# Folding low-rank factors into the weight tiles of one feed-forward, and a late place for the last out products of two others

## The chip, the cores and the metric

One core of one Trainium2 chip runs the whole program; the other cores do nothing. The metric is the time of one execution on the device in microseconds (us). It is the median over runs; the kernel before was run three times, from 2981.08 to 2985.95 us.

The engines are TensorE (PE: matrix products, with the weight loads shown apart as PEld), VectorE (DVE), ScalarE (ACT), GpSimd (POOL) and SyncE (SP, which here issues the transfers). PSUM is eight banks of 128 x 512 float32, which PE writes and DVE and ACT read.

## What is computed

The reference is a chain of eight stages over x of 8 x 128 x 512: four attentions and four feed-forwards, each with a LayerNorm ahead and a residual add behind:

```
x = x + L0_xattn(layernorm(x), ...)      stage 0
x = x + L0_ffn(layernorm(x), ...)        stage 1   (F0)
x = x + L1_xattn(layernorm(x), ...)      stage 2
x = x + L1_ffn(layernorm(x), ...)        stage 3   (F1)
x = x + L2_xattn(...); x + L2_ffn(...)   stages 4, 5
x = x + L3_xattn(layernorm(x), ...)      stage 6
x = x + L3_ffn(layernorm(x), ...)        stage 7   (F3)
```

The feed-forward of stage 1 is the one whose arithmetic is rearranged. Its hidden width is 1376 (padded to 11 blocks of 128) and the rank of its factors is 16:

```
def _lora_linear(x, w, a, b):
    base = jnp.einsum('bsd,od->bso', x, w)
    low = jnp.einsum('bsr,or->bso', jnp.einsum('bsd,rd->bsr', x, a), b)
    return base + low * SCALING          # SCALING = 2
h1 = _lora_linear(x, w1, lora_A1, lora_B1)
h3 = _lora_linear(x, w3, lora_A3, lora_B3)
g = jax.nn.silu(h1) * h3
return _lora_linear(g, w2, lora_A2, lora_B2)
```

F1 (stage 3) has 14 blocks of 128 hidden units and picks one of each 32 by a product of rank 16; F3 (stage 7) is `gelu(x @ inter_w + inter_b) @ output_w + output_b` with 16 blocks.

## The kernel before

**Data and precision.** x lies in SBUF as 8 tiles (b) of 128 x 512. A LayerNorm writes it transposed into `xnT`. Each operand of a matrix product is split into a rounded high part and the low part that is left (float32r), and a product of two such operands is three matmuls (high x high, low x high, high x low): `PASSES`, recorded at L397. So 128 x 128 weights against 512 columns, contracted over four blocks of 128, is 12 matmuls of 128x512; the 1024 columns are two halves, 24 matmuls.

**A feed-forward** (`FeedForward`, `ffn_sp`, `ffn_act`, `ffn_pool`, `ffn_pe`, `ffn_dve`) runs over chunks of 128 hidden units. For each chunk SP loads raw weight tiles of 128 x 512 into the six places of `ring`; ACT writes the high part (L1641, `ffn_act_high`) and POOL the low part (L1456, `ffn_pool_tiles`) into `w_in`, `w_kv` (two places each) or `w_out` (four places). F0 has three tiles a chunk: `in` (w1), `in2` (w3) and `out` (w2). PE makes `proj` (h1) and `score` (h3), 24 matmuls each; ACT applies silu to `proj` (L1668), DVE multiplies by `score` (L1740), and ACT and DVE split the result into `acts` (L1676, L1705). Every second chunk PE makes the out products of the two chunks before: for each of the 8 tiles of x, 6 matmuls into one of two banks `outp`, which DVE adds to x (L1700). The order on each engine is the order in which the code is written; semaphores (`m.wait(engine, event, count)`) tie the engines together.

**The low-rank part of F0 before.** `low_rank_product` multiplies A1 and A3 (loaded to `brow`, split by POOL into `w_kv[:, 1]`) with `xnT`: 24 matmuls (L413, L417) ahead of the first chunk; ACT and DVE split the result into `low_in`. Each chunk then has one more matmul for each half of `proj` (L1577) and of `score` (L1588), with the factors B1 and B3 in `low_b`. For w2, `second_low` multiplies each chunk's `acts` by A2 into two banks (L1518, 4 matmuls a chunk), and after the last chunk ACT and DVE split that sum (L1687, L1771) before each last out product gets one more matmul with B2 (L1545). The sums themselves, as L1771, wait for the last chunk.

**Around it.** `prepare_low_b` splits B1 and B3 on DVE in the first four heads of stage 0. `pe_tail`, `act_tail` and `dve_tail` are the passage from a stage to the next: the last 8 out products, the adds that also sum x (L503), squared deviations on ACT (L509), the reciprocal roots (DVE, 128x4), normalised tiles, 8 x 4 transposes (L537), and the split into `xnT`. `unread_passes` are matmuls whose result nobody reads (L593); they stand in places where PE would have nothing to do. Stage 2 starts on PE with `project_k` (L1953), which waits for normalised x from DVE (L2133).

**F1 and F3 at their end.** In F1's last chunk (13) the out products of x tiles 4 to 7 stand between `proj` and the transposes of the picks (L1599). In F3 the 8 out products of the pair before stand ahead of the last chunk's `proj` (chunk 15). The last pair's out products then open with the slot of the last chunk but one (6 matmuls for x tiles 0 and 1), and go on once the last chunk's low parts (L1705) are there.

Of the kernel before, what the change touches and what calls it, by code (L numbers as in the profile page):

```python
# [7 lines left out]
F32 = mybir.dt.float32  # L8
# [184 lines left out]
class FeedForward:  # L193


    def __init__(self, name, stage, kind, chunks, semaphores, before, small=(), row=None):
        self.name, self.stage, self.kind, self.chunks, self.row = name, stage, kind, chunks, row
        self.low_rank = kind != "gelu"
# [9 lines left out]
                      lowfull=silu, low2=2 * (kind == "silu"), low2_low=2 * (kind == "silu"),  # L208
                      low_low=4 * silu_once + 2 * pick_once, a_high=2 * silu_once + 3 * pick_once, a_split=2 * silu_once + 2 * pick_once, bmax=pick, equal=pick, weighed=pick, fmax=pick,
# [4 lines left out]
        for i in range(self.ring):  # L214
# [4 lines left out]
    NAMES = ("split high_w pre_landed pre_split small_landed sfull tfull made high low outfull added lowfull low2 "  # L219
             "low2_low low_low a_high a_split bmax equal weighed fmax picked").split() + [  # L220
# [37 lines left out]
def build(nc, ins, out):  # L258

    with ExitStack() as ctx:  # L260
# [66 lines left out]
        with nc.sbuf_tensor("low_a2", [P, 11 * 96], F32R) as low_a2, nc.sbuf_tensor("low_b2", [96, D], F32R) as low_b2:  # L327
            pass
# [38 lines left out]
        a2_raw, b2_raw = sq[:, 0:11 * 16], sq[0:96, 11 * 16:11 * 16 + D]  # L367
# [195 lines left out]
        def take_low_rank(act, A, half):  # L563
            A.events.wait(act, ("pfull", half), 1)
            if A.kind == "silu":
                act.activation(low_in[:, half * HALF:(half + 1) * HALF], proj[half][:, :], ACT.Copy, scale=2.0)\
                   .then_inc(A.events["pfree", half], 1)
                return
# [3 lines left out]
        def take_low_part(dve, A, half):  # L572
# [3 lines left out]
            if A.kind == "pick":  # L576
                dve.scalar_tensor_tensor(low_in[0:64, cols], low_in[0:64, cols].bitcast(F32), consts[0:64, C_MINUS + 1:C_MINUS + 2],
                                         proj[half][0:64, :], ALU.mult, ALU.add).then_inc(A.events["low_low"], 1)
                return
            for rows in (slice(32, 64), slice(96, 128)):  # L580
                dve.scalar_tensor_tensor(low_in[rows, cols], proj[half][rows, :], 2.0, low_in[rows, cols].bitcast(F32),
                                         ALU.mult, ALU.subtract).then_inc(A.events["low_low"], 1)

        def first_gelu_product(pe, half):

            if half == 0:
                F3.events.wait(pe, "split", F3.tile(0, 0, 0) + 1)
            pe_project_fresh(pe, F3.stage, w_in, 0, half).then_inc(F3.events["pfull", half], 1)
# [10 lines left out]
        def pe_tail(pe, n, out_of):  # L599
            for b in range(B):  # L600
                if n in LN_STAGES:
# [14 lines left out]
            for F in (F0, F1):  # L616
                if F.stage == n:
                    low_rank_product(pe, F, 0)
            if F3.stage == n:
                first_gelu_product(pe, 0)  # L620
# [7 lines left out]
        def act_tail(act, n, wait_added, first=0):  # L628
# [7 lines left out]
            for b in range(first, BH + 1):  # L636
                deviations(b)
            for b in range(2):
# [16 lines left out]
            for F in (F0, F1):  # L655
                if F.stage == n:
                    take_low_rank(act, F, 0)

        def dve_tail(dve, n, add_of):

            for b in range(BH + 1):
                add_of(b)
            if n > 7:
# [19 lines left out]
            for b in range(4, B):  # L683
                dve_ln_low(dve, n, b)


        def attention_sp(sp, A):
# [24 lines left out]
            if A.own_kv:  # L712
                sp.dma_start(sq[:, :], ins["F0_b"][:, 0:T]).then_inc(b_landed, 16)
                sp.dma_start(ring[:, 4, 0:11 * P - T], ins["F0_b"][:, T:11 * P]).then_inc(b_landed, 16)
            group(0)
# [400 lines left out]
        def attention_act(act, A):  # L1116
# [89 lines left out]
            for F in (F0, F3):  # L1206
                if F.stage == A.stage + 1:
# [1508 lines left out]
```

## Time and profile before

| | us |
|---|---|
| median of 3 runs | 2982.11 |
| lowest, highest | 2981.08, 2985.95 |
| the profiled execution: its time | 2981.35 |
| the profiled execution: its span, first to last instruction | 2979.5 |
| PE busy in the span | 2886.9 (97%) |
| DVE, ACT, POOL busy | 1705.7, 1121.6, 991.4 |
| mean granted TensorE clock, share of full | 0.998 |
| F0, from its first product to the first product of stage 2 | 889.8 to 1104.4 |

Times in the rows are microseconds from the span's start; a row of a timeline merges neighbouring instructions of one line, with their count behind an x. The last matmul's modelled end lies beyond the start of the next row, so the pace of matmuls is read from starts, not from durations. In brackets stands how long the engine had been idle and what released it.

### The profile page before, as it was taken

How to read it: one execution, taken by the hardware profiler on the slowest of the kernel's cores; microseconds unless marked ns; L12 is line 12 of the kernel's file. 1: busy time of each engine (PE TensorE's matmuls, PEld its weight loads, DVE VectorE, ACT ScalarE, POOL GpSimd, SP SyncE). 2: the span in 40 equal slices, each digit the busy share in tenths (PEclk: the TensorE clock that was granted, in tenths of full speed). 3: DMA queues.
4: the chain of work that ended last, by engine and by line, in shares of the span. 5: the costliest groups of instructions: out<-in, count | busy, mean ns of one | idle time of the engine just before them, and what ended most of it. 6: DMA issues, size and time to landing. Idle time of an engine off the chain costs nothing.

```text
span 2979.5 us, 47771 instructions
## 1 busy us (share of the span) xinstructions
PE 2886.9 (97%) x16134; PEld 2433.1 (82%) x16134; DVE 1705.7 (57%) x3462; ACT 1121.6 (38%) x3635; POOL 991.4 (33%) x830
## 2 busy tenths in 40 slices
PE   7999999999999998899999999999999999999999
PEld 6888888888888865577778888888778888888787
DVE  6545544445462249988766666666664444445644
ACT  4322222222242237732354444444443333333432
POOL 3433343423313226644333322332232333332221
PEclk9999999999999999999999999999999999999999
DMA  3111111111112111011111101110021111110111
GB/s 121 46 50 41 40 39 41 48 41 44 42 36 57 34 43 30 27 43 39 37 40 36 31 26 32 35 35 18 26 60 33 36 35 35 35 35 22 46 50 46
DMA packets 68613, 120.09 MB, mean 40 GB/s; under 512 B 8681, under 2 KB 14185, under 8 KB 68113
## 3 DMA queue, kind: packets, MB, share of 16 engines
q1 hardware_dynamic: 68498, 118.60, 13.4%
q8 instruction: 67, 1.10, 0.2%
q14 instruction: 48, 0.39, 0.0%
HBM read 116.41 MB, written 2.10 MB: 40 GB/s over the span
## 4 chain that ended last, share of the span: by engine, by line
PE 86%; DVE 8%; issue 3%; ACT 2%; POOL 1%; DMA 0%; DVEq 0%; SPq 0%; ACTq 0%; POOLq 0%
PE proj L397 40%; PE outp L397 24%; PE heado L1015 6%; PE score L974 6%; PE turn L1001 3%; PE score L397 2%; PE proj L413 1%; PE proj L941 1%; DVE blockmax L1715 1%; DVE picks L1725 1%; PE outp L1995 0%; DVE firstmax L1723 0%; PE turn L924 0%; PE proj L1958 0%; DVE acts L1705 0%
## 5 line engine op out<-in xcount | busy, mean ns | idle before, releaser
L397 PE MATMUL outp<-w_out,acts 128*128 128x512 f32 x3288 | 843.2, 400 | 13.0 <-DVE x L1700 3.9
L397 PE MATMUL proj<-xnT,w_in 128*128 128x512 f32 x3192 | 757.2, 392 | 1.3 <-ACT big L1079 1.3
L397 PEld LDWEIGHTS outp<-w_out,acts 128*128 128x128 f32 x3288 | 594.1, 188 | 144.1 <-DVE x L1700 13.0
L397 PEld LDWEIGHTS proj<-xnT,w_in 128*128 128x128 f32 x3192 | 592.6, 188 | 124.7 <-issue 1.5
L397 PE MATMUL proj<-ctxT,w_kv 128*128 128x512 f32 x1536 | 366.0, 394 | 19.8 <-POOL w_kv L731 18.6
L729 POOL TENSOR_TENSOR w_out<-ring,consts 128x512 fp32r<-128x512 f32 x96 | 102.4, 1066 | 820.9 <-PE outp L397 820.9
L397 PEld LDWEIGHTS proj<-ctxT,w_kv 128*128 128x128 f32 x1536 | 286.6, 189 | 79.1 <-issue 18.6
L1306 DVE TENSOR_TENSOR x<-x,outp 128x512 f32<-128x512 f32 x360 | 244.7, 685 | 182.2 <-PE outp L397 179.1
L1082 DVE COPY big<-proj 128x512 f32<-128x512 f32 x136 | 93.6, 688 | 343.6 <-PE proj L397 339.3
L1079 ACT ACTIVATE big<-proj 128x512 f32<-128x512 f32 x136 | 81.4, 598 | 476.4 <-PE proj L397 469.7
L729 POOL TENSOR_TENSOR w_kv<-ring,consts 128x512 fp32r<-128x512 f32 x93 | 98.0, 1053 | 464.0 <-DMA ring<-in_L_wk 445.6
L1177 ACT ACTIVATE acts<-heado 128x512 fp32r<-128x512 f32 x192 | 114.6, 597 | 309.2 <-PE heado L1015 309.2
L1312 DVE TENSOR_TENSOR acts<-heado,acts 128x512 fp32r<-128x512 f32 x192 | 132.6, 691 | 148.6 <-ACT acts L1177 148.5
L1015 PEld LDWEIGHTS heado<-ptbuf,big 128*128 128x128 f32 x1536 | 200.7, 191 | 17.8 <-ACT ptbuf L1165 1.0
L1165 ACT ACTIVATE ptbuf<-turn 128x512 f32<-128x512 f32 x192 | 114.2, 595 | 267.6 <-PE turn L1001 267.5
L1015 PE MATMUL heado<-ptbuf,big 128*128 128x128 f32 x1536 | 202.3, 274 | 1.0 <-DVE acts L1312 1.0
L974 PEld LDWEIGHTS score<-big 128*128 128x128 f32 x1536 | 184.4, 193 | 9.5 <-issue 4.7
L974 PE MATMUL score<-big 128*128 128x128 f32 x1536 | 188.9, 276 | 3.0 <-issue 1.7
L397 PE MATMUL proj<-w_kv,ctxT 128*128 128x256 f32 x1536 | 183.1, 280 | 0.9 <-DVE big L1082 0.9
L397 PEld LDWEIGHTS proj<-w_kv,ctxT 128*128 128x128 f32 x1536 | 182.0, 188 | 2.3 <-DVE big L1082 1.1
L1700 DVE TENSOR_TENSOR x<-x,outp 128x512 f32<-128x512 f32 x152 | 103.3, 685 | 89.9 <-PE outp L397 89.8
L729 POOL TENSOR_TENSOR w_in<-ring,consts 128x512 fp32r<-128x512 f32 x96 | 106.6, 1111 | 116.9 <-PE proj L397 65.8
(330 smaller groups left out, 4022.7 us busy)
## 6 DMA issues: line engine op xcount, KB each, us to landing
ring<-in_L_wq SPq DMA_DIRECT2D x96, 256.0 KB, 2.7
ring<-in_L_wo SPq DMA_DIRECT2D x96, 256.0 KB, 2.7
ring<-in_F_in SPq DMA_DIRECT2D x52, 256.0 KB, 2.7
ring<-in_L_wk SPq DMA_DIRECT2D x48, 256.0 KB, 2.7
ring<-in_L_wv SPq DMA_DIRECT2D x48, 256.0 KB, 3.4
ring<-in_F_out SPq DMA_DIRECT2D x41, 256.0 KB, 2.6
x<-in_x SPq DMA_DIRECT2D x2, 1024.0 KB, 8.4
big<-in_ctxT SPq DMA_DIRECT2D x4, 512.0 KB, 8.0
```

Of the source, the lines that this page charges most:

```text
L397: mm = pe.matmul(bank_ap, w_ap(a, c), rhs(b, c), start=first and c == 0 and n == 0, stop=last and c == chunks - 1 and n == len(PASSES) - 1)
L729: pool.tensor_tensor(dst[:, slot, 0, :], ring[:, r, :], zeros512, ALU.add).then_inc(m["high_w"], 1)
L974: mm = pe.matmul(score[half][:, b * P:(b + 1) * P], qT[:, t], kT[:, t], start=True, stop=True)
L1001: mm = pe.transpose(turn[:, b * P:(b + 1) * P], probs[j % 2][:, half, b * P:(b + 1) * P], ident)
L1015: mm = pe.matmul(heado[:, b * P:(b + 1) * P], v_pair[:, n, j % 2, :] if A.own_kv else v[:, n * S:(n + 1) * S], ptbuf[:, half, b * P:(b + 1 ...
L1079: return engine.activation(dst, src, ACT.Copy)
L1082: return engine.tensor_copy(dst, src)
L1165: act.activation(ptbuf[:, half, :], turn[:, :], ACT.Copy).then_inc(m["tfree"], 1)
L1177: act.activation(acts[:, j, 0, half * HALF:(half + 1) * HALF], heado[:, :], ACT.Copy)\
L1306: dve.tensor_tensor(x[:, b, :], x[:, b, :], outp[b % 2][:, :], ALU.add).then_inc(m["added"], 1)
L1312: dve.tensor_tensor(acts[:, j, 1, cols], heado[:, :], acts[:, j, 0, cols].bitcast(F32), ALU.subtract)\
L1700: dve.tensor_tensor(x[:, b, :], x[:, b, :], outp[b % 2][:, :], ALU.add).then_inc(m["added"], 1)
```

## The change

**F0.** The low-rank factors no longer go through the activations. PE multiplies them with each other and DVE adds twice that product to the raw weight tile in `ring` before ACT and POOL split the tile:

- `fold_in(c)`: for the tiles `in` and `in2` of chunk c, 2 x 4 matmuls of 128x128 with 64 rows; the ones for `in` use rows 0 to 63 and one bank, those for `in2` rows 64 to 127 and another bank, alternating. Four stacked copies of the rank-16 factors (high and low parts) fill the 64 rows.
- `fold_out(c)`: for the tile `out`, one matmul of 128x512 with 64 rows.
- `merge(n)`: DVE, one operation of 128x512 for each of the 33 tiles, ring = 2 x bank + ring.
- ACT's high part of a tile waits for its merge, and the three tiles are split in another place: `out` of chunk c and `in`, `in2` of chunk c + 1 behind both silus of chunk c (before: all three ahead of, or between, them, one chunk earlier for `out`).
- Gone are `low_rank_product`, `take_low_rank` and `take_low_part` for F0, the 44 extra matmuls on `proj` and `score`, `second_low` (44 matmuls) and the 8 last matmuls with B2, with their splits. `proj` of the first chunk is now made in parts as `xnT` comes in (`first_product`).
- `fold_in(0)` and the merges of the first two tiles stand in stage 0's last part; the load of A1 and A3 moves into stage 0's first group, the first three F0 tiles are loaded before stage 0's last products of values, and `prepare_low_b` has no memsets any more.
- Stage 2 gets 8 unread passes ahead of its first `project_k`.

**F1 and F3.** In F1's last chunk x tiles 6 and 7 of the pair before are made behind the transposes of the picks. In F3 x tiles 6 and 7 of the pair before are made behind the last chunk's `proj`. DVE's adds of these tiles alternate with the last low parts.

The diff, cut to its core:

```diff
+        def fold_in(pe, c):
+            m, n = F0.events, F0.tile(0, c, 0)
+            for k in range(2):
+                m.wait(pe, "merged", n + k - 1 if n else 0)
+            for i in range(DC):
+                for k in range(2):
+                    rows = slice(64 * k, 64 * k + 64)
+                    mm = pe.matmul(fold_bank(n + k)[:, i * P:(i + 1) * P], low_in[rows, i * P:(i + 1) * P],
+                                   low_b[rows, 0, c * P:(c + 1) * P], start=True, stop=True)
+                    if i == DC - 1:
+                        mm.then_inc(m["folded"], 1)
+        def fold_out(pe, c):
+            m, n = F0.events, F0.tile(0, c, 2)
+            if c == 0:
+                m.wait(pe, "a_split", 1)
+                pe.wait_ge(b_split, 5)
+            m.wait(pe, "merged", n - 1)
+            pe.matmul(fold_bank(n)[:, :], low_a2[:, c * P:(c + 1) * P], low_b2[:, :], start=True, stop=True).then_inc(m["folded"], 1)
+        def merge(dve, n):
+            m, r = F0.events, n % F0.ring
+            m.wait(dve, ("landed", r), 16 * (n // F0.ring + 1))
+            m.wait(dve, "folded", n + 1)
+            dve.scalar_tensor_tensor(ring[:, r, :], fold_bank(n)[:, :], 2.0, ring[:, r, :], ALU.mult, ALU.add).then_inc(m["merged"], 1)
...
         def pe_tail(pe, n, out_of):
+            if F0.stage == n:
...
+                fold_in(pe, 0)
...
-                        if A.kind == "silu":
-                            mm = pe.matmul(proj[half][:, :], low_b[:, 0, c * P:(c + 1) * P], low_in[:, half * HALF:(half + 1) * HALF],
-                                           start=False, stop=True)
...
+                        if A.kind == "silu" and half == int(opened):
+                            fold_out(pe, c)
                     if A.kind == "silu":
-                        if not first:
-                            second_low(*((g, j - 1) if j else (g - 1, GH - 1)))
+                        if c < A.chunks - 1:
+                            fold_in(pe, c + 1)
...
+            if A.kind == "silu":
+                m.wait(act, "merged", A.tile(g, j, k) + 1)
...
+                        for n in range(3 * c + 2, min(3 * c + 5, 3 * A.chunks)):
+                            merge(dve, n)
...
-            if j < 2:
-                dve.wait_ge(b_landed, 32)
-                dve.memset(low_b[others, i, :].bitcast(F32), 0.0).then_inc(b_high, 1)
...
+        if self.kind == "gelu" and isinstance(g, int) and GH * g + j >= self.chunks - 2:
+            return list(range(B - 2)) if j % 2 == 0 else [B - 2, B - 1]
...
+                    held = bs[2:] if A.kind == "pick" and isinstance(c, int) and c == A.chunks - 1 else []
...
+            unread_passes(pe, 8)
```

What stands in a row on PE in chunk 1 of F0 (`proj`, `score`, `turn`, `heado` are banks; `low_in` and `low_b` hold x A before and A, B after). Before:

```order
L397 MATMUL proj<-xnT,w_in 128x512 x12
L1577 MATMUL proj<-low_in,low_b 128x512
L397 MATMUL proj<-xnT,w_in 128x512 x12
L1577 MATMUL proj<-low_in,low_b 128x512
L1518 MATMUL turn<-acts,low_a 96x512 x2
L1518 MATMUL heado<-acts,low_a 96x512 x2
L397 MATMUL score<-xnT,w_kv 128x512 x12
L1588 MATMUL score<-low_in,low_b 128x512
L397 MATMUL score<-xnT,w_kv 128x512 x12
L1588 MATMUL score<-low_in,low_b 128x512
```

Now, in the same place:

```order
L399 MATMUL proj<-xnT,w_in 128x512 x12
L607 MATMUL heado<-low_b,low_a 128x512
L399 MATMUL proj<-xnT,w_in 128x512 x12
L595 MATMUL turn<-low_b,low_in 128x128
L595 MATMUL heado<-low_b,low_in 128x128
L595 MATMUL turn<-low_b,low_in 128x128
L595 MATMUL heado<-low_b,low_in 128x128
L595 MATMUL turn<-low_b,low_in 128x128
L595 MATMUL heado<-low_b,low_in 128x128
L595 MATMUL turn<-low_b,low_in 128x128
L595 MATMUL heado<-low_b,low_in 128x128
L399 MATMUL score<-xnT,w_kv 128x512 x24
```

Eight matmuls of 512 columns are gone from the chunk; one of 512 and eight of 128 columns have come, at the two boundaries inside and behind `proj`.

On DVE, at the end of stage 0 (`x,sumx<-outp,x` are the last adds, `nw_v<-sqdev` opens the reciprocal roots). Before:

```order
L1312 TENSOR_TENSOR acts<-heado,acts 128x512
L1306 TENSOR_TENSOR x<-x,outp 128x512
L503 SCALAR_TENSOR_TENSOR x,sumx<-outp,x 128x512 x5
L478 TENSOR_SCALAR nw_v<-sqdev 128x4
L433 TENSOR_SCALAR nw_t<-nw_v 128x4
```

Now:

```order
L1350 TENSOR_TENSOR x<-x,outp 128x512
L505 SCALAR_TENSOR_TENSOR x,sumx<-outp,x 128x512 x2
L614 SCALAR_TENSOR_TENSOR ring<-proj,ring 128x512
L505 SCALAR_TENSOR_TENSOR x,sumx<-outp,x 128x512
L614 SCALAR_TENSOR_TENSOR ring<-proj,ring 128x512
L505 SCALAR_TENSOR_TENSOR x,sumx<-outp,x 128x512 x2
L480 TENSOR_SCALAR nw_v<-sqdev 128x4
```

Two merges stand among the five adds ahead of the roots.

On PE at the very end of the program, F3's last four chunks. Before:

```order
L397 MATMUL outp<-w_out,acts 128x512 x48
L397 MATMUL proj<-xnT,w_in 128x512 x48
L397 MATMUL outp<-w_out,acts 128x512 x48
L397 MATMUL proj<-xnT,w_in 128x512 x24
L397 MATMUL outp<-w_out,acts 128x512 x48
```

Now:

```order
L399 MATMUL outp<-w_out,acts 128x512 x48
L399 MATMUL proj<-xnT,w_in 128x512 x48
L399 MATMUL outp<-w_out,acts 128x512 x36
L399 MATMUL proj<-xnT,w_in 128x512 x24
L399 MATMUL outp<-w_out,acts 128x512 x60
```

Twelve matmuls have moved behind the last `proj`.

## Rows read from the trace of the kernel before

**Rows 1.** The page: busy time by engine; the chain that ended last.
```profile
PE 2886.9 (97%) x16134; PEld 2433.1 (82%) x16134; DVE 1705.7 (57%) x3462; ACT 1121.6 (38%) x3635; POOL 991.4 (33%) x830
...
PE 86%; DVE 8%; issue 3%; ACT 2%; POOL 1%; DMA 0%; DVEq 0%; SPq 0%; ACTq 0%; POOLq 0%
```

**Rows 2.** Timeline of PE, 860 to 905 us: start, us, instruction, [idle before].
```profile
863.70 1.05 PE L1015 MATMUL heado<-ptbuf,big 128*128 128x128 f32 x8
864.59 0.60 PE L1001 MATMUL turn<-consts,pbuf 128*128 128x128 f32 x4
...
889.78 2.09 PE L413 MATMUL proj<-xnT,w_kv 128*128 128x512 f32 x8
...
895.34 2.88 PE L397 MATMUL proj<-xnT,w_in 128*128 128x512 f32 x12
898.06 0.39 PE L1577 MATMUL proj<-low_in,low_b 128*128 128x512 f32 x1
```

**Rows 3.** Timeline of PE, 900 to 1000 us: inside chunk 1 of F0.
```profile
913.03 0.39 PE L1577 MATMUL proj<-low_in,low_b 128*128 128x512 f32 x1
913.26 0.62 PE L1518 MATMUL turn<-acts,low_a 128*96 128x512 f32 x2
...
914.18 2.88 PE L397 MATMUL score<-xnT,w_kv 128*128 128x512 f32 x12
```

**Rows 4.** Timeline of PE, 1440 to 1540 us: F1's last chunk and its end.
```profile
1444.00 1.11 PE L1561 MATMUL score<-low_b,low_in 64*128 64x128 f32 x8
1445.04 5.73 PE L397 MATMUL proj<-xnT,w_in 128*128 128x512 f32 x24
...
1456.80 1.65 PE L397 MATMUL outp<-w_out,acts 128*128 128x512 f32 x6
1460.81 1.64 PE L397 MATMUL outp<-w_out,acts 128*128 128x512 f32 x6 [2.37 <-DVE acts L1705]
```

**Rows 5.** Timeline of PE, 1060 to 1130 us: F0's end and stage 2's start.
```profile
1091.47 0.64 PE L1518 MATMUL turn<-acts,low_a 128*96 128x512 f32 x2
...
1094.59 0.50 PE L1545 MATMUL outp<-low_b,low_in 96*128 96x512 f32 x1 [1.33 <-DVE low_in L1771]
...
1101.91 0.40 PE L1545 MATMUL outp<-low_b,low_in 96*128 96x512 f32 x1
1104.37 3.62 PE L1953 MATMUL proj<-sq,wk 128*96 128x512 f32 x4 [2.05 <-DVE sq L2133]
...
1120.23 1.09 PE L1995 MATMUL heado<-ptbuf,spread 128*64 128x128 f32 x16
1121.25 0.50 PE L1973 MATMUL score<-stacks 98*128 98x512 f32 x1
```

**Rows 6.** Groups by line, 860 to 1100 us: count, busy us, mean ns, idle before.
```profile
L503 DVE SCALAR_TENSOR_TENSOR x<-outp,x 128x512 f32<-128x512 f32 x13 | 9.0, 692 | 7.2 <-PE outp L397 5.4 <-PE outp L1545 1.7
...
L1641 ACT ACTIVATE w_in<-ring 128x512 fp32r<-128x512 f32 x11 | 6.8, 618 | 5.5 <-DMA ring<-in_F_in 5.5
...
L1456 POOL TENSOR_TENSOR w_in<-ring,w_in 128x512 fp32r<-128x512 f32 x11 | 14.4, 1306 | 53.2 <-ACT w_in L1641 53.1
```

**Rows 7.** Timeline of all engines, 1076 to 1118 us: two DVE steps.
```profile
1100.36 0.69 DVE L503 SCALAR_TENSOR_TENSOR x<-outp,x 128x512 f32<-128x512 f32 x1 [0.32 <-PE outp L1545]
...
1103.67 1.00 DVE L2133 TENSOR_SCALAR sq<-x,rstd,recentre 128x512 f32<-128x512 f32 x2
```

**Rows 8.** A stretch: us, PE, PEld, DVE, ACT, POOL busy, granted clock, DMA.
```profile
1104.30:1108.10 3.80, 3.73 (x5) 1.32 (x6) 1.19 (x3) 0.68 (x2) 0.19 (x1) 0.55 0.23 73
```

**Rows 9.** Timeline of all engines, 76 to 96 us: head 0 of stage 0.
```profile
79.56 1.23 DVE L1218 MEMSET low_b<- 64x1408 f32 x1 [0.35 <-issue]
...
87.36 5.70 PE L397 MATMUL proj<-xnT,w_in 128*128 128x512 f32 x24 [1.32 <-ACT big L1079]
```

**Rows 10.** Timeline of PE, 2915 to 2980 us: F3's end.
```profile
2963.21 1.52 PE L397 MATMUL outp<-w_out,acts 128*128 128x512 f32 x6
2965.99 1.65 PE L397 MATMUL outp<-w_out,acts 128*128 128x512 f32 x6 [1.27 <-DVE acts L1705]
```

More of the change, by code:

```diff
@@ L599, in pe_tail @@
         def pe_tail(pe, n, out_of):
+            if F0.stage == n:
+                pe.wait_ge(b_split, 4)
+                for i in range(2):
+                    LA[0].events.wait(pe, ("pfree", i), LA[0].projections * NG)
+                fold_in(pe, 0)
             for b in range(B):
+                if F0.stage == n and b == B - 1:
+                    F0.events.wait(pe, "merged", 2)
                 if n in LN_STAGES:
@@ L662, in dve_tail @@
                 add_of(b)
+                if F0.stage == n and b in (1, 2):
+                    merge(dve, b - 1)
             if n > 7:
@@ L1445, in chunks, with ffn_pool_tiles @@
                           .then_inc(m["landed", slot], 16)
+                    if A.kind == "silu" and c == 0:
+                        LA[0].events.wait(sp, "pv", 2 * NH)
+                        for dst, src in A.small:
+                            sp.dma_start(dst, src).then_inc(m["small_landed"], 16)
             ffn_run(sp, A, chunks)
-        def ffn_pool_tiles(pool, A, g, j):
+        IN_TILES = ("in", "in2")
+        def ffn_pool_tiles(pool, A, g, j, kinds=None):
             m = A.events
             for k, what in enumerate(A.what):
+                if kinds and what not in kinds:
+                    continue
                 r = (len(A.what) * j + k) % A.ring
@@ L1508, in ffn_pe @@
             pre = int(A.low_rank)
-            def second_low(g, j):
-                c = GH * g + j
-                for half in range(2):
-                    m.wait(pe, "low", 2 * c + half + 1)
-                    if c == 0:
-                        m.wait(pe, "a_split", 1)
-                    for k in range(2):
-                        mm = pe.matmul(ln_banks[half][0:96, :], low_a2[:, c * 96:(c + 1) * 96],
-                                       acts[:, j, k, half * HALF:(half + 1) * HALF], start=c == 0 and k == 0,
-                                       stop=c == A.chunks - 1 and k == 1)
-                    mm.then_inc(m["lowfull"], 1)
             def out_product(p, slots, bs, last):
@@ L1535, in out_product @@
                     m.wait(pe, "added", B * p + (b - 1))
-                    more = last and A.kind == "silu"
                     if opened and b < 2:
@@ L1539, in out_product @@
                     else:
-                        mm = pe_out(pe, b, slots, last=not more)
-                    if more:
-                        if b == 0:
-                            m.wait(pe, "low2_low", 2)
-                            m.wait(pe, "a_split", 2)
-                        mm = pe.matmul(outp[b % 2][:, :], low_in[0:96, b * S:(b + 1) * S], low_b2[:, :], start=False, stop=True)
+                        mm = pe_out(pe, b, slots)
                     mm.then_inc(m["outfull"], 1)
@@ L1656, in chunks @@
                     more = not (isinstance(c, int) and c == A.chunks - 1)
-                    for what in A.what[:-1] if more else ():
+                    for what in A.what[:-1] if more and A.kind != "silu" else ():
                         ffn_act_high(act, A, *after(g, j), what)
@@ L1669, in chunks @@
                            .then_inc(m["pfree", half], 1)
-                    if more:
+                    if A.kind == "silu":
+                        ffn_act_high(act, A, g, j, "out")
+                        for what in IN_TILES if more else ():
+                            ffn_act_high(act, A, *after(g, j), what)
+                    elif more:
                         ffn_act_high(act, A, *after(g, j), "out")
@@ L1757, in chunks @@
                         low_part(c, j, half)
+                        if closing:
+                            add(p, adds[half])
                     if A.row is not None and isinstance(c, int) and c < 3:
                         add_row(dve, A.row, (range(0, 4), range(4, 6), range(6, 8))[c])
-                    for b in adds[BH:]:
+                    for b in adds[BH:] if not closing else ():
                         add(p, b)
```

197 lines of the change are left out of this document (86 added, 111 removed).

## The prediction, made before the changed kernel was run

> **What bounds the kernel now.** I read the page first: PE is busy 97% of the span and holds 86% of the chain that ended last [rows 1], so nearly every matmul counts at its pace, and a gain elsewhere counts only where PE waits for it. Next the timeline of PE through F0: from 895 to 1091 us its rows follow each other without an idle bracket (three of them in [rows 3]). The pace comes from starts: 12 matmuls of 512 columns take 895.34 to 898.06, which is 2.72, or 0.227 each [rows 2]; one low-rank matmul between two blocks costs 913.03 to 913.26, which is 0.23 [rows 3]. Then the passages, where PE does wait: at F0's end [rows 5], at F1's end [rows 4], at F3's end [rows 10], and in head 0 of stage 0 [rows 9]. The groups by line give the other engines' single steps: 0.69 for a DVE pass from PSUM, 0.62 for ACT's high part, 1.31 for POOL's low part [rows 6].
>
> **What leaves PE in F0.** (a) 44 matmuls on `proj` and `score` at 0.23: 10.1. (b) `second_low`: 4 matmuls take 913.26 to 914.18, 0.92 [rows 3]; ten of the eleven stand inside the chunks: 9.2. The eleventh belongs to (d). (c) `low_rank_product`: 24 matmuls from 889.78 to 895.34 [rows 2]: 5.6. The first chunk's `proj` takes its place as `xnT` comes in, at the same pace, so this is a clean loss of 24 matmuls. Together 24.9.
>
> **What comes to PE in F0.** Nothing in the trace is exactly `fold_in`: eight matmuls of 128 columns with 64 rows, alternating between the lower and upper rows. The row nearest in shape is L1561, also 64 rows and 128 columns, but always the same rows: eight take 1444.00 to 1445.04, 1.04 [rows 4], where eight full ones take 863.70 to 864.59, 0.89 [rows 2]. So narrowing the array and going back costs 0.15 in the burst, and the first wide matmul behind such a burst has 0.50 in its row instead of 0.39 [rows 5]: 0.26 in all. The row nearest in its alternation is L1995: two halves of the columns by turns, sixteen in 1120.23 to 1121.25, 1.02 [rows 5], the time of eight. So halves of the array did run at once there. `fold_in` has separate banks for its two halves, so I take that pace: eight in 0.51, plus 0.11 behind it and the switching, which halves less than the work: 0.8. The bounds are 0.5 (pure pace, switching hidden) and 1.2 (1.04 + 0.11, no overlap). Eleven of them: 8.8, from 5.5 to 13. `fold_out` is one wide matmul with its own switching, 0.23 + 0.3 = 0.53, from 0.23 to 0.8: eleven make 5.8, from 2.5 to 9. Added 14.6; net in F0's body, 24.9 - 14.6 = 10.3 gained.
>
> [...]
>
> **What the other engines must carry.** The 33 merges on DVE are 33 x 0.69 = 23 us; DVE is busy 57% [rows 1], so this is free if each lands in time. Let E be the end of a chunk's second `proj` half. By then `out` is merged, since its fold stood 2.7 earlier. The fold of `in` ends at about E + 0.8, its merge at E + 1.7 and that of `in2` at E + 2.4; ACT makes the high parts of out, in, in2 by E + 1.4, 2.3 and 3.0 (0.62 each); POOL the low parts by E + 2.7, 4.0 and 5.3 (1.31 each). PE asks for `in` after `fold_in` and 24 matmuls, at E + 0.8 + 5.5 = E + 6.3, and for `in2` at least 5.5 later. The slack is 2.3 where no out product stands between, and 11 more where one does. In the first chunk the factors of w2 must be there too; POOL splits them while the transposes run. So nothing is added. At the end of stage 0 `fold_in(0)` pays its 0.8 (counted); the two merges fall between adds that PE paces at six matmuls, 1.36, and a pair of add and merge is 1.38. ACT's two high parts there only change places with the squared deviations.
>
> **F0's end (d).** Before, the last group of 48 ends at T = 1091.47; the eleventh `second_low`, a wait of 1.33 for DVE, and eight products follow with 1.05 each (1094.59 to 1101.91 in seven steps) [rows 5]. Stage 2's first matmul starts at T + 12.9 [rows 5]. That start hangs on DVE: the sixth add starts at 1100.36 [rows 7] and PE 4.0 later. Now the first add can start at about T + 1.4 (DVE still has the former pair's add of tile 7 and a small mask operation). Three matmuls instead of four take 0.23 out of a loop of two tiles, so a tile takes 0.93. The sixth add then starts at about T + 6.0 and stage 2 at T + 10.0: 2.9 gained. The 8 unread passes run from about T + 7.5 for 1.8 and end before that start; they cost nothing unless the start came earlier than T + 9.3.
>
> **The clock (g).** [...]
>
> **Stage 0's head 0 (h).** DVE's memset of 1.23 stands ahead of the score operations whose maximum ACT waits for, and PE then waits 1.32 for ACT [rows 9]. Without the memset DVE is 1.2 earlier; I count 1.1, from 0 to 1.3. The 256 KB more to load there stand behind transfers that are needed first. The later memset, in head 1, hides behind 120 matmuls.
>
> **F1 and F3 (i).** F1: PE waits 2.37 for the last low parts [rows 4]. Twelve matmuls, 2.7, now stand behind the transposes. But DVE must do two more adds between the low parts, and PE's next product in the same bank waits for the add of tile 7. Counted through, the products of the last slot start at about 1459.6 instead of 1460.81: 1.2, from 0.4 to 2.4. F3: the wait is 1.27 [rows 10]. With twelve matmuls behind `proj`, the same add holds the second opening product; the last slot starts at 2965.5 instead of 2965.99: 0.5, from 0 to 1.3. What is late next is the add, not the low part.
>
> **The sum.** 10.3 + 2.9 + 1.6 + 1.1 + 1.2 + 0.5 = 17.6 off the profiled execution's 2981.35 (a span of 2979.5 and 1.85 around it), 2963.8. The median of the runs lies 0.8 above that execution, so 2964.5.
>
> **The rivals.**
> - *No overlap of the row halves, or the clock stays low.* `fold_in` costs 1.2 instead of 0.8, 4.4 more; or 1.6 of the clock is not had; or the 4.5 of (d) and (g) is lost again, since stage 2's first blocks also wait for mask rows, which SP loads only behind F0's last out product. For: the only 64-row row runs one after another. Against: L1995. Any one of them gives 2966 to 2969, 2969 as its typical time.
> - *The tiles come late.* The chain fold, DVE, ACT, POOL now has to run between two `proj`s. POOL's mean is 1.31, and were its three operations slowed by DVE's merges to over 2.0, or ACT held by a silu that waits, PE would stand at each of ten chunk boundaries. At 0.8 each: 8 more, 2972.5. Against: the slack of 2.3, and PE never waited for a tile of F0 before.
> [...]
> - *More than that.* Switching hidden and `fold_in` at 0.5, `fold_out` at 0.3, F1's full 2.4: 5 to 7 less, 2958.5.
> - *It does not do what it says.* The matmuls leave but PE waits somewhere in F0 for as long: about 2979. The unbroken rows of F0 speak against any such second bound near.
>
> **How the numbers follow.** The forecast, 2964.5 with 2961 to 2967 around it: 0.46. No overlap or no clock: 0.22. Late tiles: 0.10. More: 0.13. Nothing much gained: 0.05. Slower: 0.04. From 2957 to 2974 holds the first four but for their far ends, over 0.8. About 0.2%, 6 us, is what a measurement of this kernel can tell from no change: faster than 2976 has 0.90, within it 0.06, slower 0.04.
>
> **What would show it.** In the profile after: `fold_in` rows of eight in about 0.6 from first start to the next wide matmul's, with pairs nearly on one start; 1.0 or more says no overlap. No idle bracket on `proj` in F0, and POOL's low part of `in` ending some 2 ahead of it. F0's body (first product to the end of the last 48) shorter by about 11 than 201.7. T to stage 2's first matmul about 10, with a granted clock near 1. The wait of 1.32 in head 0 gone; about 0 to 0.7 idle at the ends of F1 and F3. Idle brackets on `proj` or on `fold_in` itself, waiting for POOL or for a merge, would make the prediction wrong, and so would a wide matmul behind each fold that starts a microsecond late.

## The result: slower by 0.68%, where a gain of 0.6% was forecast

| | before | changed |
|---|---|---|
| median of 4 runs, us | 2982.06 | 3002.89 |
| lowest, highest | 2981.08, 2985.95 | 3001.8, 3004.6 |
| the profiled execution's span | 2979.5 | 3000.6 |
| mean granted clock | 0.998 | 0.992 |

The ratio is 1.0068, 95% interval 1.0056 to 1.008. The forecast was 2964.5, its range 2957 to 2974, so the kernel is 38 us slower than forecast and outside the range.

The page of the changed kernel: busy time by engine, two DMA queues (packets, MB, share), the chain that ended last.

```profile
PE 2889.2 (96%) x16121; PEld 2430.0 (81%) x16121; DVE 1726.9 (58%) x3488; ACT 1122.4 (37%) x3631; POOL 988.4 (33%) x819
...
q8 instruction: 67, 1.10, 0.1%
q14 instruction: 74, 0.61, 0.1%
...
PE 83%; DVE 9%; issue 4%; ACT 2%; DMA 0%; DVEq 0%; POOL 0%; SPq 0%; ACTq 0%; POOLq 0%
```

PE has 13 matmul records fewer than in [rows 1] and is yet busy 2 us longer, and its share of the chain falls from 86% to 83%. So PE waits more, and more of its work runs at the lower of the two clocks that the trace records, 0.50 (the mean is 0.992 instead of 0.998). The line on queue 14 will matter: these are transfers of instructions, 48 in the kernel before and 74 now.

Where the 21 us come from is read by laying the same rows of both traces side by side:

| row of PE, start in us | before | changed | ahead (-) or behind (+) |
|---|---|---|---|
| stage 0's tail products | 872.24 | 872.77 | +0.5 |
| F0's first product | 889.78 | 897.60 | +7.8 |
| stage 2's first matmul | 1104.37 | 1099.06 | -5.3 |
| F1's first product | 1276.26 | 1267.94 | -8.3 |
| a `proj` block behind stage 4's loop | 2026.54 | 2048.73 | +22.2 |
| the last 36 products | 2967.80 | 2988.53 | +20.7 |

The change works where it was made: F0 and stage 2 give back 7.8 and bring 8.3 more, which is 16. Two other stretches take more than that. One is the passage from stage 0 into F0 (7.3), which the change touches. The other is stage 4's loop (30.5 between F1's first product and the row behind it), in which the change edits no line. "Stage 4's loop" is the piece of each engine's program that is run six times in stage 4, with five jumps back to its start.

**F0 itself** looks as forecast. The timeline of PE in F0's second chunk:

```profile
913.65 0.50 PE L607 MATMUL heado<-low_b,low_a 64*128 64x512 f32 x1
914.08 3.02 PE L399 MATMUL proj<-xnT,w_in 128*128 128x512 f32 x12
917.03 0.32 PE L595 MATMUL turn<-low_b,low_in 64*128 64x128 f32 x1
917.03 0.33 PE L595 MATMUL heado<-low_b,low_in 64*128 64x128 f32 x1
...
917.41 0.27 PE L595 MATMUL turn<-low_b,low_in 64*128 64x128 f32 x1
917.42 0.27 PE L595 MATMUL heado<-low_b,low_in 64*128 64x128 f32 x1
917.62 5.75 PE L399 MATMUL score<-xnT,w_kv 128*128 128x512 f32 x24
```

`fold_in` has its pairs on one start, and from its first start to the next wide matmul there are 0.59 us. `fold_out` takes 0.43 (913.65 to 914.08). None of these rows has an idle bracket; within F0 only the very first `fold_in` waits, 0.95 at 904.70.

These two figures are not yet the whole cost, because the wide products beside a fold are slower too: the twelve behind `fold_out` take 2.95 (914.08 to 917.03), where twelve in the kernel before take 2.76 (910.27 to 913.03). The whole chunk, from one `proj` to the next, has everything in it. Before and changed:

```profile
907.27 2.92 PE L397 MATMUL proj<-xnT,w_in 128*128 128x512 f32 x12
920.13 2.92 PE L397 MATMUL proj<-xnT,w_in 128*128 128x512 f32 x12
```

```profile
910.84 2.88 PE L399 MATMUL proj<-xnT,w_in 128*128 128x512 f32 x12
923.21 2.88 PE L399 MATMUL proj<-xnT,w_in 128*128 128x512 f32 x12
```

That is 12.86 and 12.37, so a chunk is 0.49 shorter. The forecast's prices give 0.92 + 0.92 - 0.8 - 0.53 = 0.51.

**The passage into F0.** Timelines of the changed kernel from 877 us on: first POOL, then DVE, then PE.

```profile
878.00 1.30 POOL L1506 TENSOR_TENSOR w_kv<-ring,w_kv 128x512 fp32r<-128x512 f32 x1
879.26 2.52 POOL L1522 TENSOR_TENSOR low_a<-big,consts 64x1408 fp32r<-64x1408 f32 x1
881.86 3.16 POOL L1525 TENSOR_TENSOR low_a<-big,low_a 32x1408 fp32r<-32x1408 f32 x1
```

```profile
877.31 0.69 DVE L505 SCALAR_TENSOR_TENSOR x<-outp,x 128x512 f32<-128x512 f32 x1 [0.69 <-PE outp L399]
...
878.04 1.29 DVE L480 TENSOR_SCALAR nw_v<-sqdev 128x4 f32<-128x4 f32 x1
879.37 2.45 DVE L435 TENSOR_SCALAR nw_t<-nw_v 128x4 int32<-128x4 int32 x1
881.85 0.17 DVE L437 TENSOR_SCALAR rstd<-nw_t 128x4 int32<-128x4 int32 x1
882.05 2.99 DVE L443 TENSOR_TENSOR nw_t<-rstd,nw_v 128x4 f32<-128x4 f32 x1
885.08 0.16 DVE L445 SCALAR_TENSOR_TENSOR nw_t<-nw_t,rstd 128x4 f32<-128x4 f32 x1
```

```profile
879.73 1.07 PE L619 MATMUL proj<-ctxT 128*128 128x512 f32 x4
887.49 2.93 PE L399 MATMUL outp<-w_out,acts 128*128 128x512 f32 x6 [6.69 <-DVE x L505]
```

And the first of the roots, and the same six products, in the kernel before:

```profile
877.73 0.17 DVE L478 TENSOR_SCALAR nw_v<-sqdev 128x4 f32<-128x4 f32 x1 [0.23 <-ACT ptbuf L509]
880.95 1.65 PE L397 MATMUL outp<-w_out,acts 128*128 128x512 f32 x6 [0.67 <-DVE x L503]
```

Three DVE operations on four columns take 1.29, 2.45 and 2.99, where their neighbours of the same size take 0.16 or 0.17. Each ends when the POOL operation beside it ends: 879.33 and 879.30, 881.82 and 881.78, 885.04 and 885.02. The two 64- and 32-row operations of POOL are the new split of w2's factor. They stand under the one chain that PE waits for: PE waits 6.69 instead of 0.67 for its six products, and they take 2.93 instead of 1.65, at a granted clock of 0.50 (887.45 to 890.42) instead of 1.00. 6.0 and 1.3 are the 7.3 of the table.

**Stage 4's loop.** First the longest waits of PE in the whole span and one line of DVE's waits (us in total, times, longest), then DVE and PE in the first turn that waits.

```profile
PE outp L399 <- DVE x L1350: 21.9, 10, 4.0
PE proj L399 <- POOL w_kv L774: 18.8, 1, 18.8
PE outp L399 <- DVE x L505: 9.1, 11, 6.7
...
DVE pbuf L1295 <- issue: 29.6, 5, 6.0
```

```profile
1660.02 0.17 DVE L447 SCALAR_TENSOR_TENSOR rq<-heado,rq 128x8 f32<-128x8 f32 x1
1666.22 1.13 DVE L1295 SCALAR_TENSOR_TENSOR pbuf<-score,rq,maskadd 128x128 f32<-128x128 f32 x4 [6.03 <-issue]
```

```profile
1671.07 2.93 PE L399 MATMUL outp<-w_out,acts 128*128 128x512 f32 x6 [3.99 <-DVE x L1350]
```

"issue" says that DVE waited for nothing that the profile shows. It happens five times, some 86 us apart, each time the loop jumps back to its start, and PE then waits up to 4.0 for the add that stands behind. PE's longest waits from 1640 us to the loop's end, before and changed:

```profile
PE turn L950 <- DVE big L1295: 3.8, 5, 0.8
```

```profile
PE outp L399 <- DVE x L1350: 19.4, 5, 4.0
```

The clock falls as well. In the stretches 1660 to 1746 and 1746 to 1832 the granted clock is 0.96 and 0.98, where a stretch of the same length in the kernel before has 1.00. Over the loop the trace has 24 us at a clock of 0.50, against none before. That half of them is lost is my estimate from the 0.50: 19.4 + 12 is the 30.5, within 1. The DMA view has the likely reason. Between 1655 and 2030 queue 14 moves 24 blocks of instructions of 8192 bytes, where the kernel before moves none. Five belong to each of the five turns behind a jump (in the first at 1660.8, 1661.6, 1664.2, 1666.9 and 1710.7; the twenty-fifth comes at 2054.2), which is all but one of the 26 that the page has more.

### The profile page after: what moved, and what is told of

It reads as the page before. It is cut to its first block, busy times and chain, and to the rows that moved or that the text cites. A ratio compares the mean times of both kernels' runs of the same rounds, so it can differ in the third digit from the quotient of the medians.

```text
span 3000.6 us, 47794 instructions
## 1 busy us (share of the span) xinstructions
PE 2889.2 (96%) x16121; PEld 2430.0 (81%) x16121; DVE 1726.9 (58%) x3488; ACT 1122.4 (37%) x3631; POOL 988.4 (33%) x819
## 4 chain that ended last, share of the span: by engine, by line
PE 83%; DVE 9%; issue 4%; ACT 2%; DMA 0%; DVEq 0%; POOL 0%; SPq 0%; ACTq 0%; POOLq 0%
PE proj L399 38%; PE outp L399 24%; PE heado L1058 6%; PE score L1017 5%; PE turn L1044 3%; PE score L399 2%; PE proj L415 1%; DVE x L1720 1%; DVE blockmax L1735 1%; DVE picks L1745 1%; DVE pbuf L1295 0%; PE outp L2012 0%; DVE firstmax L1743 0%; ACT acts L1220 0%; DVE acts L1356 0%
## 5 line engine op out<-in xcount | busy, mean ns | idle before, releaser
L399 PE MATMUL outp<-w_out,acts 128*128 128x512 f32 x3288 | 849.4, 402 | 36.5 <-DVE x L1350 21.9
L399 PE MATMUL proj<-ctxT,w_kv 128*128 128x512 f32 x1536 | 366.7, 395 | 19.7 <-POOL w_kv L774 18.8
L399 PEld LDWEIGHTS proj<-ctxT,w_kv 128*128 128x128 f32 x1536 | 287.1, 189 | 79.2 <-issue 18.8
L1506 POOL TENSOR_TENSOR w_out<-ring,w_out 128x512 fp32r<-128x512 f32 x41 | 56.1, 1367 | 311.3 <-ACT w_out L1662 311.3
```

The lines of the kernel that those rows point to most:

```text
L399: mm = pe.matmul(bank_ap, w_ap(a, c), rhs(b, c), start=first and c == 0 and n == 0, stop=last and c == chunks - 1 and n == len(PASSES) - 1)
```

## The experiments

Two theories came from this reading. **Contention**: POOL's new operations hold DVE in the passage, some 7 us. **Place of code**: stage 4's loop stands later in DVE's program, because 26 instructions were added in F0, and at its new place it must be loaded again at every jump back, some 28 us. The rival of both is that stage 4, or the passage, waits for something else that the change does.

To move code without anything else I add one-element memsets on DVE, spread over F0's chunks, on a tile of their own:

```
+        pad = sb("pad", [1, 16])
...
+                    if A is F0:
+                        for i in range(102 * (c + 1) // 11 - 102 * c // 11):
+                            dve.memset(pad[0:1, i:i + 1], 0.0)
```

Below, "N memsets" is this edit with N for 102 (and a wider tile where N is large). Each takes 59 ns, beside PE's work.

### 102 memsets in the changed kernel

> The changed kernel with 102 memsets of one element on DVE, spread over F0's eleven chunks, on a tile that nobody reads. With the 26 instructions that the change itself adds, everything behind F0 stands 128 instructions later in DVE's program than in the kernel before, instead of 26. Theory (place of code): the five waits of about 6 us on DVE in stage 4's loop come from 8 KB transfers of instructions that the loop needs at its new place and did not need at its old one; moved by 128, it has them no longer: the ten idle brackets on PE before `outp` go, about 28 us less, near 2975. Rival (stage 4 waits for data, or for something else that the change moved): the waits stay, 3002 to 3004; the memsets themselves cost under 1 us on either.

2973.21 (2971.18 to 2974.76); ratio to the kernel before 0.9966, interval 0.9953 to 0.9978. A hundred useless instructions made the changed kernel 30 us faster. The waits are gone: queue 14 has 49 transfers, no DVE group waits for "issue", and PE waits 2.5 in all for the adds of attention (L1351) instead of 21.9.

```profile
q14 instruction: 49, 0.40, 0.0%
```

```profile
PE outp L400 <- DVE x L1351: 2.5, 5, 0.9
```

### 26 memsets in the kernel before

> The kernel before, nothing of the change in it, with 26 such memsets in F0. Theory (place of code): stage 4's loop now stands where it stands in the changed kernel, so DVE waits five times some 6 us in it, and the time is 2982 + 28 = 3010. Rival: nothing in stage 4 depends on the place of code, 2981 to 2984.

2980.56 (2977.96 to 2987.42), against 2983.38 for the kernel before on this chip; ratio 0.9994, interval 0.9985 to 1.0004. No waits in stage 4, 48 transfers on queue 14. By my count the loop now stood where it stands in the changed kernel, so this **went against the theory**. The mistake was in the count. In these compiled programs an instruction that waits for two or three semaphores stands as two or three, and the changed kernel has more of these. In DVE's the loop (266 instructions) begins at number 1717 before, at 1743 here, and at 1776 in the changed kernel: 59 later than before, 26 by operations and 33 by instructions that only wait.

### POOL's split of w2's factor later

```
                 m.wait(pool, "small_landed", 32)
+                pool.wait_ge(ln_normed, dve_count(1, 6))
```

> The changed kernel, but POOL waits, ahead of its operations on w2's small factors and on F0's first low parts, until DVE has gone through the roots of the normalisation. Theory (the passage from stage 0 to F0): DVE's operations of 128x4 take 0.17 again instead of 1.3 to 3.0, PE's wait of 6.69 ahead of F0's first product goes to near 0, F0's first product starts 7 to 8 us earlier against the last product of stage 0, and the time is 6 to 8 less, about 2996. Against it: the small factors of w2 come later, and if PE waits for them at the first fold of the out product, some of it is lost again; below 2 us gained in all would say that. Rival (DVE is late there for another reason, such as its two new merges): DVE's roots stay long, 3001 to 3004.

2996.7 (2994.08 to 2996.82), 6.2 less than the changed kernel; ratio 1.0046, interval 1.0029 to 1.0062. In the timelines of POOL, DVE and PE of this run:

```profile
887.14 2.53 POOL L1523 TENSOR_TENSOR low_a<-big,consts 64x1408 fp32r<-64x1408 f32 x1 [10.31 <-DVE pbuf L518]
```

```profile
875.56 1.28 DVE L480 TENSOR_SCALAR nw_v<-sqdev 128x4 f32<-128x4 f32 x1
876.88 0.17 DVE L435 TENSOR_SCALAR nw_t<-nw_v 128x4 int32<-128x4 int32 x1
```

```profile
879.89 1.66 PE L399 MATMUL outp<-w_out,acts 128*128 128x512 f32 x6 [1.57 <-DVE x L505]
```

With nothing moved but POOL's two operations and the tile operations behind them, the DVE operation that took 2.45 takes 0.17, the wait of 6.69 is 1.57, and the six products take 1.66 at a granted clock of 1.00. What is left, 1.28 on L480, stands beside POOL's tile operation of `w_kv` (875.52 to 876.82). Nothing of the gain is lost again at the first `fold_out`. The intervals of the two ratios, 1.0056 to 1.008 without POOL's wait and 1.0029 to 1.0062 with it, just overlap; the rows carry the reading. That the two engines got in each other's way, and not DVE's two new merges, which this run keeps, is shown as the cause of this loss. The five waits of 6 us stay (30.4 in all), as they must.

### Both edits

> The 102 memsets and POOL's wait together. If both losses are what I take them for and have nothing to do with each other: 3003 - 28 - 7 = 2968, below the kernel before by 14 and near the forecast of 2964.5. If they share a cause, less than the sum of the two.

2967.82 (2962.63 to 2969.16); ratio 0.9946, interval 0.9929 to 0.9962. Forecast from the sum of the two losses: 2968. Each takes away what it took away alone, so the two losses are independent. Without them the kernel is 15.6 below the kernel before on this chip (2983.38); the forecast was 17.6.

### 59 memsets in the kernel before

> The kernel before with 59 memsets of one element on DVE in F0. In the compiled programs of DVE the extra instructions that hold a second or third wait count too: there the changed kernel stands 59 behind the kernel before, not 26. Stage 4's loop, 266 instructions long, begins at number 1717 in the kernel before, 1743 with 26 memsets, 1878 in the changed kernel with 102 (all three without the waits) and 1776 in the changed kernel (with them). Here it begins at 1776 too. Theory (place of code, counted so): five waits of about 6 us on DVE in stage 4's loop, 8 KB transfers of instructions in it, and 28 us more than the kernel before: 3010. Rival (the loop waits for something that the changed kernel does, and the 102 memsets hid it by chance): no waits, 2982 to 2984.

3014.86 (3011.73 to 3018.84); ratio 1.0106, interval 1.0087 to 1.0126. The kernel before, with not one of its own lines changed, is 32 us slower when its loop begins where the changed kernel's does. Its page's row on queue 14, its waits and DVE's first turn:

```profile
q14 instruction: 74, 0.61, 0.1%
```

```profile
DVE pbuf L1252 <- issue: 31.1, 5, 6.7
```

```profile
1669.94 0.17 DVE L446 SCALAR_TENSOR_TENSOR rq<-heado,rq 128x8 f32<-128x8 f32 x1
1675.93 1.13 DVE L1252 SCALAR_TENSOR_TENSOR pbuf<-score,rq,maskadd 128x128 f32<-128x128 f32 x4 [5.82 <-issue]
```

These are the changed kernel's rows over again. The place alone makes the loss. This is shown, together with the version with 49 memsets below, whose loop stands ten instructions earlier and does not wait.

### Where the bad places are

Three versions ask for the limits of the bad places. The first two add 24 and 12 memsets to the changed kernel with POOL's wait, the third 49 to the kernel before.

> The changed kernel with POOL's wait and 24 memsets instead of 102: stage 4's loop begins at 1800 and ends at 2065. In blocks of 128 instructions (8 KB) that is 14.06 to 16.13, against 13.88 to 15.95 in the changed kernel. Theory (a loop that needs one block more than DVE's store holds, with some few instructions ahead of the program that the compiled file does not have): the loop is at the start of a block again, the waits are gone, 2968. Rival (any place behind some point is bad until far on): waits of 6 us stay, 2996.

> The same with 12 memsets: the loop begins at 1788 and ends at 2053, 13.97 to 16.04. One look for where the bad places end. If a loop is bad when it touches a fourth block, and 7 to 15 instructions stand ahead of what the compiled file shows, this one is good, 2968; if those instructions are none or few, or if the chip loads ahead and is caught by that, it is bad, 2996 with the five waits.

> The kernel before with 49 memsets: stage 4's loop begins at 1766 and ends at 2031, ten instructions earlier than with 59. Theory (266 instructions touch a fourth block of 128 from only ten places in 128; with 7 to 15 instructions that stand ahead of what the compiled file shows, this place is not one of them): no waits on DVE in stage 4, 2982 to 2984. Rival (the bad places are a wide range that 12 memsets more than the changed kernel's place happen to end): waits of 6 us, 3012.

24 memsets: 2965.64 (2963.17 to 2968.77), ratio 0.9943, interval 0.9925 to 0.9961, no waits. It is **the fastest version of the study**, 17 us below the kernel before. Its lead over the other versions without the two losses (2965.64 against 2966.35 to 2967.82) is within their scatter. Its waits of PE, longest first, have neither of the two losses (the 18.8 stands at the program's start, where the kernel before waits 18.6):

```profile
PE proj L400 <- POOL w_kv L775: 18.8, 1, 18.8
PE proj L1987 <- DVE stacks L2168: 7.7, 8, 2.6
PE turn L994 <- DVE big L1340: 6.4, 8, 1.1
PE outp L400 <- DVE x L1722: 5.5, 16, 1.2
```

12 memsets: 2967.57 in its one run, no waits. 49 in the kernel before: 2989.36 in one run, 7.6 above the median of the kernel before there and inside neither figure that I had given, but with no wait on DVE in stage 4 and 48 transfers on queue 14. So its 7.6 are not this loss; what they are stays open. The profiled run of the version with 26 memsets was 2987.42 where the median was 2980.6, so a single run can be off by as much.

### The unit in which places repeat

> The kernel before with 187 memsets in F0, 128 more than the 59 that made it slow: stage 4's loop begins at 1904. It asks for the unit in which places repeat. Unit of 128 instructions, 8 KB, the size of one transfer of instructions in the trace (the loop is bad when it touches four of them): bad again, five waits of 6 us, 3012 to 3015. Unit of 256, 16 KB (bad when it touches three of them, as 1776 and 2032 would and 1904 would not): no waits, 2982 to 2986. The 187 memsets are 59 ns each, 11 us of DVE spread over F0's 190, beside PE's work.

> The same with 315 memsets, 256 more than 59: the loop begins at 2032. Either unit says bad: waits of 6 us on DVE in stage 4, 3012 to 3018 in this one look. No waits would say that the places don't repeat by blocks at all, and that something else decides.

187 memsets: 3015.43 (3012.77 to 3016.1), ratio 1.0109, interval 1.009 to 1.0128, waits of 29.7 in five. 315: 3021.67 in its one run, waits of 30.2 in five. All places of the loop that were tried (1766, 1788 and 2032 in one run each):

| loop begins at | in blocks of 128 | waits in stage 4 |
|---|---|---|
| 1717 (before) | 13.41 | none |
| 1743 | 13.62 | none |
| 1766 | 13.80 | none |
| 1776 (changed; 59 in before) | 13.88 | 5 of 6 us |
| 1788 | 13.97 | none |
| 1800 | 14.06 | none |
| 1878 | 14.67 | none |
| 1904 | 14.88 | 5 of 6 us |
| 2032 | 15.88 | 5 of 6 us |

The bad range lies between 1766 and 1788, less than 22 places wide, and came back at both places tried, 128 and 256 further on. That much the table shows. The rest is an estimate of mine from these places. I take 128 instructions to a block, since the bad places come back by 128; the whole program's transfers of 8192 bytes on queue 14, 74 with 59 memsets, are 75 with 187 and 77 with 315. 266 instructions are 10 more than two blocks, and they touch a fourth block from 9 places in 128 only (a loop that begins at place 119 of a block is the first). That fits all nine places, if 7 to 15 instructions stand ahead of what the compiled program shows: a turn of a loop of three blocks then brings no transfer, and a turn of one of four brings five (between 1655 and 2030 none in the kernel before, 24 in the changed kernel). Why five and not four is not shown, and neither are the 7 to 15.

Blocks of 256 do not fit: by them the place 1904 would be as harmless as 1788, and it was slow by 33 us (3015.43, against 2982.46 for the kernel before on that chip). The stall at each jump is about 6.0 at all three bad places: 29.6 to 31.1 in five.

### Without the eight unread passes

```
-            unread_passes(pe, 8)
```

> The changed kernel with POOL's wait and 102 memsets, without the 8 unread passes that PE makes at the end of F0. What the passes bring by my sum is 1.6 us: without them the first K projections of stage 2 run at half the clock (3.6 for the four instead of 2.0) and the time is 1 to 2 above 2968. Rival (the low clock only comes later, as the windows in stage 2 show, and the passes bring nothing): within 0.5 of 2968 and stage 2's later milestones at the same distance.

2966.35 (2966.22 to 2968.11); ratio 0.9946, interval 0.9929 to 0.9962, like the version with them (2967.82). In the two timelines of PE, first without the passes, then with them:

```profile
1091.60 3.51 PE L1975 MATMUL proj<-sq,wk 128*96 128x512 f32 x4 [2.27 <-DVE sq L2155]
```

```profile
1089.10 1.99 PE L620 MATMUL proj<-ctxT 128*128 128x512 f32 x8
1091.46 1.96 PE L1975 MATMUL proj<-sq,wk 128*96 128x512 f32 x4 [0.37 <-DVE sq L2156]
```

The passes do what I said for the four records: 1.96 at a granted clock of 1.00 instead of 3.51 at 0.54. But the stretch from stage 2's first matmul to F1's first product takes 171.8 without them (1091.60 to 1263.36) and 173.0 with them (1091.46 to 1264.43); in the version with 24 memsets it is 169.8 (1092.12 to 1261.87). The stretches at 0.50 fall elsewhere in stage 2: in all they last 7 us there without the passes, and from 3 to 17 us in the versions with them. So neither of my two figures is shown. No gain appears in the time, and one of 1.6 could not have been seen.

### fold_in row by row

```
-            for i in range(DC):
-                for k in range(2):
-                    rows = slice(64 * k, 64 * k + 64)
+            for k in range(2):
+                rows = slice(64 * k, 64 * k + 64)
+                for i in range(DC):
```

> The changed kernel with POOL's wait and 102 memsets, but fold_in makes its four products of the lower 64 rows first and then its four of the upper, instead of by turns. Same instructions, same number. Theory (by turns the two halves of the rows run at once, 0.6 from fold_in's first start to the next wide matmul): in this order they don't, the burst takes 1.0 to 1.1, and eleven bursts cost 4 to 5 more: 2967.8 + 4.5 = 2972. Rival (the halves overlap in any order, or the pace does not come from them): 0.6 a burst, 2968.

2966.38 (2963.64 to 2969.72); ratio 0.995, interval 0.9933 to 0.9967. The timeline of PE:

```profile
910.00 0.32 PE L596 MATMUL turn<-low_b,low_in 64*128 64x128 f32 x1
910.01 0.33 PE L596 MATMUL heado<-low_b,low_in 64*128 64x128 f32 x1
...
910.38 0.27 PE L596 MATMUL turn<-low_b,low_in 64*128 64x128 f32 x1
910.40 0.27 PE L596 MATMUL heado<-low_b,low_in 64*128 64x128 f32 x1
910.60 5.74 PE L400 MATMUL score<-xnT,w_kv 128*128 128x512 f32 x24
```

My theory fell. The burst takes 0.60 (910.00 to 910.60), as by turns. The four products of the upper rows are written behind the four of the lower, and start beside them all the same, 0.01 to 0.02 later. The halves of the rows overlap (the premise of the forecast's 0.8), and writing them by turns is not needed for it.

## Why the prediction was wrong, point by point

- **Terms (a), (b), (c) and the folds** were right taken together: a chunk is 0.49 shorter, forecast 0.51. The bursts alone, 0.59 and 0.43, look cheaper than the 0.8 and 0.53 of the sum, but the wide products beside them carry the rest. F0's body, from its first product to the end of the last 48, takes 191.7 instead of 201.7, so it is 10.0 shorter; forecast 11.1. The difference is the wait of 0.95 for the first merges, at `fold_in(1)` in the first chunk, which I had at nothing.
- **Term (d)**: stage 2's first matmul comes at T + 9.8, with T at 1089.3; forecast T + 10.0.
- **Term (g), the clock**: no run shows the sum's 1.6. The K projections take 1.96 at a granted clock of 1.00 instead of the 3.62 of [rows 5] at 0.53 (0.55 over the stretch of [rows 8]), but the kernel without the passes is as fast (2966.35 against 2967.82). The stretches at 0.50 that lay at 1104 and 1125 lie at 1106 and 1120 in the changed kernel, as long in all as before.
- **Term (h), head 0**: in the two profiles the wait for ACT went from 1.32 [rows 9] to 0.93, and the stretch from the 24 K products to it shrank by 0.4 (8.40 to 8.00), not 1.1; the first cast behind the memset runs over 128 rows now and takes 1.19 instead of 0.69. But this stretch varies between runs. In the six traces of the kernel before and its versions it is 7.5 to 9.2, 8.7 in the mean, in the eight of the changed kernel 6.9 to 8.0, 7.7 in the mean. So the gain is about 1.0 and the term was right.
- **Term (i)**: F1's last slot. From the last chunk's 24 `proj` products to the 30 last out products there are 16.47 (1439.90 to 1456.37) instead of 17.60 (1445.04 to 1462.64): 1.1, forecast 1.2. F3, from its last 48 `proj` products to the last 36: 30.97 (2957.56 to 2988.53) instead of 32.06 (2935.74 to 2967.80): 1.1, forecast 0.5. What is late there is the add, as said (0.17 twice).
- **The step that failed first**: "POOL splits them while the transposes run. So nothing is added." I asked only whether the split is in time for its reader, not beside what else it runs. The two operations on 1408 columns ended up under the chain of roots, not under the transposes, held DVE there, and cost 6.2 by the third experiment.
- **The step that was missing**: "The 33 merges on DVE are 33 x 0.69 = 23 us" and "this is free". The DVE instructions that the change adds were costed by their time and not by their place. Nothing in the sum and none of the rivals had it; it cost 30 by the first experiment, most of the 38 us between forecast and result. "Slower" was given 0.04, and not for this: for bursts dearer than taken, which use up the 17.6 from 17.6 / 22 = 0.8 a burst on. The chunk's 0.49 against 0.51 shows nothing of that size.

The sum itself, 17.6, is roughly borne out once both losses are away: the four versions without them that were run several times are 15.4 to 17.1 below the kernel before on their chips. The terms as read here, 10.0 + 3.1 + 1.0 + 1.1 + 1.1, less 0.6 for the `fold_in` in stage 0 and 0.9 that is left in the passage (17.54 before, 18.42 with 24 memsets, from the 30 tail products to F0's first), make 14.8. So that the best version comes within 0.5 of the 17.6 is partly luck.

## What to carry to other kernels

An edit in one stage can cost in a loop that it doesn't touch, here 30 us of 3000. When instructions come or go ahead of a loop of a few hundred, count its place in the compiled program, with the instructions that only wait, and look at the transfers of instructions inside the loop; "idle, waiting for issue" each time the loop jumps back was their mark here, up to 6.7 on DVE, and a few empty instructions ahead of the loop tell within one run. When work moves to an idle engine, ask what else runs at that time and whom it can hold, and not only whether its own reader gets it in time: here two POOL operations of 2.52 and 3.16 cost 6.2 beside a short DVE chain that PE waited for, and behind that chain no wait at the first `fold_out`.

## What the hardware showed that I had not expected

- The loop of 266 DVE instructions cost 6 us more at each jump back when it began at 1776, 1904 or 2032, which are 128 apart, and had no such wait from the six other places tried, 1766 and 1788 among them.
- Three DVE operations on four columns (their neighbours of the same size take 0.16 or 0.17) that started 0.04 to 0.19 behind a long POOL operation lasted until that one ended: 1.29 and 2.45 (TENSOR_SCALAR) and 2.99 (TENSOR_TENSOR). An add with one operand from PSUM kept its length: 0.69 at 877.31, beside POOL's operations of 876.75 to 879.30.
- The products on the lower and upper 64 rows overlapped even when four of one half were written ahead of four of the other: 0.60 for eight, in either order.
